# Rounding the gate's input in two halves, and a last attention group ordered by key tile

## The reference

```python
r = x                                   # and k = v = fside
x = x + attention(bi_wkv(x, fside, fside, w1, u1, cond), w_qkv, w_o)
x = x + ffn(bi_wkv(x, fside, fside, w2, u2, cond), w_gate, w_up, w_down)

# bi_wkv: two linear scans over the tokens (forward and backward) of exp(k)*v and exp(k),
#         their quotient, times sigmoid(r)
# attention: 16 heads of 32 channels, causal softmax(q k^T / sqrt(32)) v, then w_o
# ffn: _mx_linear(silu(gate) * up, w_down), gate = _mx_linear(x, w_gate), up = _mx_linear(x, w_up)
# _mx_linear: the input is rounded to a small float (6 bits, clipped at 7.5) with one
#             power-of-two scale per block of 32 channels; the weights likewise (clipped at 6)
```

## Time and profile before

| | us |
|---|---|
| median of 3 runs (range) | 857.79 (857.45 to 858.77) |
| the profiled execution | 857.56 |
| its span, first to last instruction | 855.8 |
| PE busy | 734.1 (86%) |
| DVE busy | 752.2 (88%) |
| ACT busy | 507.1 (59%) |

### The profile page before, as it was taken

One profiled execution on the slowest core, in us unless ns is written; L12 is line 12 of the kernel. 1 busy time (PEld: TensorE's weight loads), 2 busy tenths in 40 slices (PEclk: granted clock), 3 DMA queues, 4 the chain that ended last, 5 costly groups with the idle time before them and its releaser, 6 DMA issues.

```text
span 855.8 us, 10886 instructions
## 1 busy us (share of the span) xinstructions
PE 734.1 (86%) x4001; PEld 388.3 (45%) x4001; DVE 752.2 (88%) x1070; ACT 507.1 (59%) x754; POOL 72.4 (8%) x149
## 2 busy tenths in 40 slices
PE   3676567699789999998899999988999999999785
PEld 1222223355444444554544444554434445567674
DVE  4999999999999879999998799999997899744887
ACT  4966656367875466468773663687736637453440
POOL 1000000201100002111000021110000211200000
PEclk9676787799999999999999999999999999999998
DMA  9723210556300004764010045660100266500001
GB/s 321 280 98 111 92 68 13 116 125 178 75 22 29 1 12 99 209 163 122 13 38 1 13 99 159 164 166 16 38 1 13 63 142 179 122 1 1 2 2 49
DMA packets 31253, 73.06 MB, mean 85 GB/s; under 512 B 5857, under 2 KB 6881, under 8 KB 29409
## 3 DMA queue, kind: packets, MB, share of 16 engines
q1 hardware_dynamic: 18304, 44.57, 17.3%
q0 software_dynamic: 6144, 16.79, 8.2%
q10 hardware_dynamic: 6752, 11.02, 4.3%
HBM read 34.61 MB, written 4.19 MB: 45 GB/s over the span
## 4 chain that ended last, share of the span: by engine, by line
DVE 50%; PE 30%; issue 12%; ACT 4%; DMA 2%; POOL 1%; ACTq 0%; DVEq 0%; POOLq 0%
PE bank L1636 10%; DVE negmax L1085 6%; DVE num L991 3%; DVE fn L977 3%; PE bank L1393 3%; PE bank L1652 2%; PE bank L1528 2%; PE bank L1401 2%; PE bank L1428 2%; PE bank L1472 2%; DVE den L1015 2%; DVE num L1017 2%; DVE ratio L1124 2%; DVE den L1002 2%; DVE num L1005 1%
## 5 line engine op out<-in xcount | busy, mean ns | idle before, releaser
L1401 PE MATMUL bank<-h,wqkv 128*128 128x512 f32 x256 | 116.7, 608 | 0.0
L589 ACT ACTIVATE region<-bank 128x384 f32<-128x384 f32 (+1 forms) x192 | 92.3, 529 | 39.4 <-PE bank L1475 37.3
L1085 DVE TENSOR_REDUCE negmax<-bank 128x4 f32<-128x512 f32 (+2 forms) x96 | 97.6, 1034 | 15.5 <-PE bank L1431 10.7
L1472 PE MATMUL bank<-stacks 128*128 128x512 f32 (+3 forms) x256 | 102.3, 407 | 6.7 <-ACT region L589 5.2
L1428 PE MATMUL bank<-stacks 128*128 128x128 f32 (+3 forms) x256 | 77.0, 393 | 16.8 <-DVE negmax L1085 14.5
L1474 PE MATMUL bank<-maxrow,pick 128*128 128x512 bf16 (+3 forms) x256 | 79.9, 312 | 0.0
L339 POOL DMA_DIRECT2D stacks<-rounded_rows x64 | 34.6, 549 | 521.6 <-DVE ratio L1124 322.8
L1401 PEld LDWEIGHTS bank<-h,wqkv 128*128 128x128 f32 x256 | 49.4, 196 | 57.0 <-issue 56.1
L1393 PE MATMUL bank<-wqkv,h 128*128 128x512 f32 x128 | 61.1, 621 | 4.7 <-DVE h L1025 4.7
L1472 PEld LDWEIGHTS bank<-stacks 128*128 128x128 f32 x256 | 49.4, 193 | 26.1 <-ACT region L589 12.3
L1428 PEld LDWEIGHTS bank<-stacks 128*128 128x128 f32 x256 | 45.7, 200 | 27.8 <-DVE negmax L1085 19.3
(11 more groups left out here) (197 smaller groups left out, 1551.6 us busy)
## 6 DMA issues: line engine op xcount, KB each, us to landing
stacks<-rounded_rows POOLq DMA_DIRECT2D x64, 128.0 KB, 5.5
stacks<-rows SPq DMA_DIRECT2D x64, 128.0 KB, 2.7
stacks<-rows POOLq DMA_DIRECT2D x64, 128.0 KB, 2.7
kt<-in_fside ACTq DMA_DIRECT2D x30, 256.0 KB, 3.2
stacks<-rounded_rows SPq DMA_DIRECT2D x48, 128.0 KB, 5.5
region<-in_w_gate SPq DMA_DIRECT2D x4, 1024.0 KB, 11.4
h<-in_x SPq DMA_DIRECT2D x4, 1024.0 KB, 4.9
xt<-in_x SPq DMA_DIRECT2D x4, 1024.0 KB, 4.8
```

Source lines behind the costliest of these rows:

```text
L589: nc.scalar.activation(probs[:, i, P_AT[tiles[0]]:P_AT[tiles[0]] + columns], key_bank(g, n)[:, 0:columns], ACT.Exp, scale=SCALE).then_inc( ...
L1085: nc.vector.tensor_reduce(o, scored, AX_X, ALU.max, negate=True).then_inc(max_taken, 1)
L1401: mm = nc.tensor.matmul(qk_banks(g)[s][:, :], wqkv[:, j, C * s + P * g:C * s + P * g + P], h[:, j, :], start=(j == 0), stop=(j == CJ - 1), ...
L1472: nc.tensor.matmul(o, ks[s][:, i, P * t:P * t + P], qs[s][:, i, P * t:T], start=True, stop=False, skip_group_check=True)
```

## The change

Two edits.

The gate's input is rounded in two pairs of channel tiles (0 and 1, then 2 and 3) in turns 0 to 2: three instructions over 128x1024 for each pair instead of three over 128x2048, with two more `carry` writes, and one `xq_ready` after each pair. PE does step f = 0 in two passes: after the first pair, the products with channel tiles 0 and 1 for all four feature tiles (eight products into four banks), and after the second pair those with tiles 2 and 3. The clamp of the first pair goes to a free row of `rows`, that of the second to the upper half of the old place. Waits on `xq_ready` elsewhere count two per turn.

In the last group of every turn (g = 3), the twelve units are ordered by key tile over all heads: four units of tile 0, four of tile 1, four of tiles 2 and 3. `weigh_values` waits in this group for four exponentials before key tile 0, for eight before tile 1 and for all twelve before tile 2. Its wait for `normed` stays in front.

```diff
+        def key_unit(g, n):
+
+            if g == GROUPS - 1:
+                return n % HG, KEY_TILES[n // HG]
+            return n // PER_HEAD, KEY_TILES[n % PER_HEAD]
...
             def exps(b, g, first, last):
                 for n in range(first, last):
-                    i, tiles = n // PER_HEAD, KEY_TILES[n % PER_HEAD]
+                    i, tiles = key_unit(g, n)
...
             def sizes(b, f):
...
-                    act.wait_ge(xq_ready, b + 1)
+                    act.wait_ge(xq_ready, 2 * b + 2)
...
+        def round_pair(ch, k, clamped):
+
+            pair = slice(2 * k, 2 * k + 2)
+            carry()
+            ch.link(nc.vector.tensor_tensor(q8[:, pair, :], ratio2[:, pair, :], over(inv[:, :], 2), ALU.mult, saturate=False))
+            carry()
+            ch.link(nc.vector.tensor_scalar(clamped, q8[:, pair, :], E2M3_MAX / 64, -E2M3_MAX / 64, ALU.min, ALU.max))
+            return nc.vector.tensor_tensor(xq[:, pair, :], clamped, over(scale_b[:, :], 2), ALU.mult)
...
                 act_scales(qc, BLOCK // CJ)
-                round_acts(qc, ratio2[:, :, :], xq).then_inc(xq_ready, 1)
+                round_pair(qc, 0, top2).then_inc(xq_ready, 1)
+                round_pair(qc, 1, q16[:, 2:4, :]).then_inc(xq_ready, 1)
...
             def scores_by_key(b, g, n):
 
-                s, i, tiles = g % 2, n // PER_HEAD, KEY_TILES[n % PER_HEAD]
+                s, (i, tiles) = g % 2, key_unit(g, n)
...
                     else:
                         pe.wait_ge(v_copied, b * TT + TT)
-                    pe.wait_ge(p_ready, b * (GROUPS * UNITS) + g * UNITS + UNITS)
+                    if g < GROUPS - 1:
+                        pe.wait_ge(p_ready, b * (GROUPS * UNITS) + g * UNITS + UNITS)
                 for t in range(first, last):
+                    if g == GROUPS - 1 and t < PER_HEAD:
+                        pe.wait_ge(p_ready, b * (GROUPS * UNITS) + g * UNITS + HG * (t + 1))
...
-                pe.wait_ge(xq_ready, b + 1)
-                for f in range(FJ // 2):
+                for pair in range(2):
+                    pe.wait_ge(xq_ready, 2 * b + 1 + pair)
+                    for o, w, done in ((0, gate_q, gate_ready), (2, up_q, up_ready)):
+                        for i in range(2):
+                            for j in (2 * pair, 2 * pair + 1):
+                                mm = nc.tensor.matmul(bank[o + i][:, :], w[:, j, P * i:P * i + P], xq[:, j, :],
+                                                      start=(j == 0), stop=(j == CJ - 1), skip_group_check=True)
+                        if pair:
+                            mm.then_inc(done, 1)
+                for f in range(1, FJ // 2):
...
-QUANT_STEPS = 31
+QUANT_STEPS = 33
```

More of the change, by code:

```diff
@@ L616, in part_sizes @@
                 else:
-                    act.wait_ge(xq_ready, b + 1)
+                    act.wait_ge(xq_ready, 2 * b + 1)
                 nc.scalar.activation(size[:, :, columns_of(part)], inter[:, 2 * f:2 * f + 2, columns_of(part)], ACT.Abs,
@@ L1520, in part_gate_up @@
                 if f == 0:
-                    pe.wait_ge(xq_ready, b + 1 + part)
+                    pe.wait_ge(xq_ready, 2 * b + 1 + part)
                 if n >= 2:
```

## The result

The changed kernel takes 851.86 us (median of 4 runs, 851.75 to 852.59) against 857.62: a ratio of 0.9937, interval 0.9925 to 0.9948. The profiled execution has a span of 850.2 us against 855.8, 5.6 us less.

A forecast was written before the change was run, and what follows sets the result against it. At the start of gate and up PE waits 1.16 us for DVE's rounding, then PE is the bound. 857.56 - 3.45 - 0.7 = 853.41 us, or 853.6 us against the median; range 852.4 to 856.7 us.

The forecast's parts named there:

- the low end of the range: Whole kernel: bounds allow 853.0 us at the lowest; with room for runs up to 0.3 us below median, 852.4 us.
- The pairs: Gate's step 0, turns 0 to 2: PE starts early on the first rounded pair, gaining 1.15 us per turn, 3.45 us altogether.
- DVE's late start: Gate and up: rounding in pairs takes DVE 0.47 us longer; the first product moves by 0.47 us only, costing nothing.
- Rival B: Gate and up: DVE sets the pace, so 0.47 us counts fully in every turn; 858.5 to 859.2 us, chance 0.10.
- the rule that the prediction cites from the Trainium skill: DVE's rounding: many small tiles each pay the latency between instructions; by that alone each turn loses 0.47 us.
- The key order: Last group's weighing: zero in turns 0 to 2, held by the normalisation; 0.7 us gained in the last turn.
- rival C: Last group: the key order gains nothing anywhere, as ACT paces the last turn's new order; 854.3 us, chance 0.13.

The follow-up runs named there:

- The second set: The changed kernel run once more with no edit: median 852.93 us, ratio 0.9940 to the kernel before.
- norm_early: The changed kernel with the third group's normalisation moved ahead of one scan on DVE: ratio 0.9950 to the kernel before.
- wait_fill: `wait_both` with eight filler products, results never used, in PE's wait ahead of step 0: ratio 1.0001 to the kernel before.
- wait_both: The changed kernel, but PE's first pass waits for both pairs like the second: ratio 1.0061 to the kernel before.
- keys_only: The kernel before with only the order by key tile, old rounding and step 0 in one pass: ratio 1.0015, executions from 856.52 to 863.29 us.

## Why the prediction was wrong

The mechanism held at each step; two sizes did not.

**The step that failed is the low end of the range: 0.3 us for the runs.** The prediction took 853.0 us as the lowest that its bounds allow, and went on for the runs: "the runs of the kernel before lie up to 0.3 us below their median: with some room 852.4". That was the spread of three runs. In the larger sets executions of the kernel before lie up to 1.55 us below their median (855.86 for 857.41, 27 executions). Two places that the change does not touch differ from trace to trace. The first normalisation of turn 0 lies anywhere from 210.13 to 212.49 us, earliest in the profiled execution after, 1.13 us ahead of the one before; the second trace after was 0.14 us ahead and its span 4.5 us shorter, not 5.6. And PE's two waits for a DMA in the last turn took 0.20 to 1.34 us.

The terms as measured, 3.81 + 0.72 us off 857.6, give 853.1 us, which is inside the range. The four executions of the first comparison lay around 851.9 us. For the one with a trace it is the head; the other three have none, so for them this is argued and not shown. The second set, at 852.93 us on median, would have been inside the range, and `norm_early`, which gains by its trace what the change gains, was 4.2 us faster than before, so that the first set fell so low is put down to chance.

**The pairs, forecast 1.15, measured 1.26 us in turn 0**, beyond the 1.17 us that the prediction took as the most. "It is free again at 286.54 + 0.49 = 287.03": here a row's end was taken for the end of PE's slot. The first product of the early pass starts 0.34 us behind the start of that same row (285.41 and 285.75), since the rows of successive products overlap. PE was idle 0.15 us longer than I counted, and the early pass starts that much sooner. The second pass starts at 287.54, 0.06 us after the eight products would have let it (285.75 + 1.73). The rounding ends at 287.48, as predicted (288.61 less the lead of 1.13): the second pair came just as the first pass was through, and not 0.1 us ahead.

**DVE's late start** cost nothing, as said: the first product moved from 291.93 to 290.25, earlier by 0.55 us net of the head (forecast 0.47), and the last one still waits 1.63 us for PE. Rival B, or the rule that the prediction cites from the Trainium skill taken alone, would have cost 0.47 us per turn; `wait_fill` shows that price where PE has no early pass, 0.49 us.

**The key order** did nothing in turns 0 to 2 and gained 0.72 us in the last, forecast 0.7. The sign named for rival C, new idle time in the last group's scores, did come up in turns 0 to 2 (0.44 us for 0.08), where the normalisation hides it. In the last turn, where C would have cost, it did not, and C fell: ACT's exponentials end at 768.43, 0.6 us behind the start of the weighing, and PE does not notice.

**The prediction missed** that the wait it removed held a second risk: two kernels with a similar (1.24 us) or longer wait (1.63 us) lost the clock there.

## What to carry to other kernels

An engine's wait for a chain of elementwise work can be filled with the half of its products whose operand comes first, as long as the sum over the contraction may stay open in several banks; the gain ends where the second half becomes late, which was just the case here. Where an idle engine has two or three chains ending near it, freeing one can gain nothing (`norm_early`), and two edits together more than the sum of each: 1.0 us per turn, for 0 and 0.35. And a difference of one or two microseconds is to be read between events on either side of the change, not from the ends of two executions, and an idle time next to a missing row from what ended it and from the weight loads.

## What the runs showed of the hardware

PE's granted clock fell behind an idle stretch of about 1.63 us in `wait_both`, in each of three turns, at a cost of about 1.6 us each; eight products with no use restored it. With 1.2 us idle it held in one execution of `keys_only` and fell in another. The first inputs of the changed kernel landed 0.73 us apart in two traces, and up to 1.93 us apart over fourteen traces of kernels with the same head.
